# One ring of four PSUM banks for the maximum tiles and the side jobs, and whole value products between groups of tiles, in an attention and feed-forward kernel

## The reference, cut to what matters

```python
hid = _group_norm(xr, norm_w, norm_b)                      # 32 groups
qkv = jnp.einsum('oc,bcl->bol', qkv_w, hid) + qkv_b[None, :, None]
...
weight = jnp.einsum('bhct,bhcs->bhts', q * scale, k * scale)
weight = jax.nn.softmax(weight.astype(jnp.float32), axis=-1)
a = jnp.einsum('bhts,bhcs->bhct', weight, v)
h = jnp.einsum('oc,bcl->bol', proj_w, a.reshape(b, c, L)) + proj_b[None, :, None]
x = x + h.reshape(b, c, hh, ww)
...
h = gelu(rmsnorm2d(x, norm1_w)); x = x + conv1x1(h, conv_w, conv_b)
h = rmsnorm2d(x, norm2_w);       h = gelu(conv1x1(h, ffn_w1, ffn_b1))
x = x + conv1x1(h, ffn_w2, ffn_b2)
```

## Time and profile before

| | |
|---|---|
| median of 3 runs | 1712.55 us (1711.57 to 1712.57) |
| the profiled execution | 1714.98 us, its span 1713.0 us |
| mean granted TensorE clock | 0.984 |
| TensorE busy (matmuls) | 1675.6 us, 98% |
| VectorE busy | 1460.5 us, 85% |
| ScalarE busy | 1367.4 us, 80% |
| GpSimd busy | 337.3 us, 20% |

### The profile page before, as it was taken

The page is one execution under the profiler, slowest core; times in us unless marked ns, Lnnn a source line. Parts: engine busy times, 40 slices in busy tenths (PEclk is TensorE's granted clock), DMA queues, the critical chain, the costliest instruction groups (busy, mean ns, idle before and its releaser), DMA issues.

```text
span 1713.0 us, 33562 instructions
## 1 busy us (share of the span) xinstructions
PE 1675.6 (98%) x12522; PEld 678.8 (40%) x12522; DVE 1460.5 (85%) x2415; ACT 1367.4 (80%) x2478; POOL 337.3 (20%) x411
## 2 busy tenths in 40 slices
PE   5999999999999999999999999999999999899999
PEld 2433333333333333333333333333333333455555
DVE  4999999999999999999999999999999995455552
ACT  2388888888888888888888888888888888666664
POOL 3101111111111111212121212121211113222220
PEclk9699999999999999999999999999999998999999
DMA  6133333333333334343333333233333320333332
GB/s 117 27 46 58 58 58 59 58 58 58 57 59 55 61 54 62 52 62 54 61 55 59 57 58 58 46 59 46 58 45 58 46 60 21 94 104 96 102 109 74
DMA packets 58625, 106.16 MB, mean 62 GB/s; under 512 B 32864, under 2 KB 33632, under 8 KB 58464
## 3 DMA queue, kind: packets, MB, share of 16 engines
q1 hardware_dynamic: 56160, 95.64, 32.7%
q10 hardware_dynamic: 2304, 8.39, 1.3%
HBM read 34.48 MB, written 9.05 MB: 25 GB/s over the span
## 4 chain that ended last, share of the span: by engine, by line
PE 96%; DVE 2%; SPq 0%; issue 0%; POOL 0%; ACT 0%; DMA 0%; DVEq 0%; POOLq 0%; ACTq 0%
PE psum L696 33%; PE psum L667 27%; PE psum L680 14%; PE psum L773 7%; PE psum L578 4%; PE psum L744 2%; PE psum L746 2%; PE psum L745 2%; PE psum L570 2%; PE psum L623 2%; DVE maxes L1022 1%; PE psum L781 1%; PE psum L591 0%; PE psum L601 0%; DVE k_high L1112 0%
## 5 line engine op out<-in xcount | busy, mean ns | idle before, releaser
L1022 DVE TENSOR_REDUCE maxes<-psum 128x1 f32<-128x512 f32 x2048 | 1276.8, 683 | 93.7 <-PE psum L667 91.7
L915 ACT ACTIVATE probs<-psum 128x512 f32<-128x512 f32 x2048 | 1110.0, 597 | 218.1 <-PE psum L680 194.5
L667 PE MATMUL psum<-k_stack,q_stack 62*128 62x512 f32 x2048 | 771.3, 456 | 1.7 <-DVE maxes L1022 0.9
L680 PE MATMUL psum<-q_stack,k_stack 64*128 64x512 f32 x2048 | 752.8, 452 | 0.0
L696 PE MATMUL psum<-probs,values 128*32 128x256 f32 (+1 forms) x7040 | 624.7, 427 | 0.7 <-ACT probs L915 0.6
L667 PEld LDWEIGHTS psum<-k_stack,q_stack 62*128 62x128 f32 x2048 | 317.0, 187 | 506.8 <-DVE maxes L1022 421.4
L680 PEld LDWEIGHTS psum<-q_stack,k_stack 64*128 64x128 f32 x2048 | 305.1, 185 | 12.3 <-issue 6.1
L696 PEld LDWEIGHTS psum<-probs,values 128*32 128x32 f32 x7040 | 138.7, 108 | 317.0 <-issue 232.6
L773 PE MATMUL psum<-probs,first_weights 128*128 128x512 f32 x256 | 116.6, 598 | 0.9 <-DVE raw L1190 0.9
L434 POOL CAST parts<-neg_max 128x16 fp32r<-128x16 f32 x64 | 12.6, 197 | 528.3 <-DVE neg_max L1001 528.3
L924 ACT ACTIVATE probs<-psum,params_sb 128x512 f32<-128x512 f32 x128 | 82.1, 686 | 20.9 <-PE psum L746 14.7
(11 more groups left out here) (95 smaller groups left out, 965.9 us busy)
## 6 DMA issues: line engine op xcount, KB each, us to landing
q_stack<-q_high SPq DMA_DIRECT2D x128, 128.0 KB, 3.9
k_stack<-k_high SPq DMA_DIRECT2D x128, 128.0 KB, 5.2
values<-inv_rms_rows SPq DMA_DIRECT2D x32, 512.0 KB, 5.0
x_sb<-in_x SPq DMA_DIRECT2D x16, 512.0 KB, 7.2
q_stack<-q_low SPq DMA_DIRECT2D x64, 128.0 KB, 6.3
k_stack<-k_low SPq DMA_DIRECT2D x64, 128.0 KB, 7.0
q_stack<-rows SPq DMA_DIRECT2D x512, 2.0 KB
attn<-raw SPq DMA_DIRECT2D x128, 64.0 KB, 2.3
```

Source lines behind the costliest of these rows:

```text
L667: nc.tensor.matmul(psum[:, BANKS + tile % BANKS, :], q_stack[used, place, p, chunk % 4, chunk // 4, :], k_stack[used, place, p, HALF * key ...
L680: nc.tensor.matmul(psum[:, tile % BANKS, :], k_stack[used, place, p, 128 * chunk:128 * chunk + 128], q_stack[used, place, p, :, t, :], sta ...
L915: nc.scalar.activation(probs[:, tile % 8, :], psum[:, tile % BANKS, :], ACT.Exp, scale=SCALE).then_inc(probs_ready, 1)
L1022: nc.vector.tensor_reduce(maxes[:, chunk // 4, j, 4 * p + chunk % 4, key_half:key_half + 1], psum[:, BANKS + max_tile(u, s, k) % BANKS, :] ...
```

## The change

The side jobs lose bank 7 of their own. Banks 3, 4, 5 and 7 become one ring of four, and M tiles and side jobs take its places in the order in which TensorE issues them (`max_place`, `job_place`); each waits for whatever reads the place four before. S tiles keep their three banks. In `slot` the order of a step is now one of four, by `s % 4`; side jobs keep their steps and stand behind two pairs at odd steps. The value product is whole in three of four orders and split in the fourth (`s % 4 == 3`). On ScalarE a side job's copy moves from behind the fourth exponential to behind the second. Before the first M tile TensorE now waits for the copies of image 1's first products (`c == PROLOGUE - 1`). The diff, cut to its core:

```diff
+        RING_BANKS = (3, 4, 5, 7)
+        max_place, job_place, freed = {}, {}, []
+        def side_job_read(b, half, s):
+            at = (half, s)
+            if at == LAST_K and PROLOGUE <= b + 1 < IMAGES:
+                return qk_full, 4 * (b + 1) + 4
...
+            return None
+        for u in range(-1, UNITS):
+            for s in range(STEPS):
+                for k in range(4):
+                    if k == 2 and u >= 0 and side_job_read(u // 2, u % 2, s) is not None:
+                        job_place[u // 2, u % 2, s] = len(freed)
+                        freed.append(side_job_read(u // 2, u % 2, s))
+                    if 0 <= max_tile(u, s, k) < UNITS * TILES:
+                        max_place[max_tile(u, s, k)] = len(freed)
+                        freed.append((max_taken, max_tile(u, s, k) + 1))
+        def bank_of(n):
+            return psum[:, RING_BANKS[n % len(RING_BANKS)], :]
+        def job_bank(b, half, s):
+            return bank_of(job_place[b, half, s]) if b >= 0 else misc
...
+                if c >= PROLOGUE:
+                    wait_for_place(job_place[(c - 1, *VALUES[part])])
                 for k in range(4):
                     chunk = 4 * part + k
-                    last = nc.tensor.matmul(misc[:, 128 * k:128 * k + 128], hid[:, 128 * chunk:128 * chunk + 128],
-                                            wv[:, :], start=True, stop=True)
+                    last = nc.tensor.matmul(values_bank(c, part)[:, 128 * k:128 * k + 128],
+                                            hid[:, 128 * chunk:128 * chunk + 128], wv[:, :], start=True, stop=True)
                 last.then_inc(v_ready, 1)
...
-                if (half, s) == VALUES[0] and b + 1 >= PROLOGUE and has_image(b + 1):
-                    if has_image(c):
+                if (half, s) == GROUP_VAR and has_image(c):
+                    pe.wait_ge(gn_mix, b + 3)
+                    if b >= 0:
+                        wait_for_place(job_place[b, half, s])
+                    else:
                         pe.wait_ge(mean_taken, b + 3)
-                    values_of(b + 1, 0)
-                if (half, s) == GROUP_VAR and has_image(c):
-                    at_least(pe, mean_taken, b + 3)
-                    at_least(pe, v_full, b * 2 + 3)
-                    pe.wait_ge(gn_mix, b + 3)
-                    nc.tensor.matmul(misc[:, 0:1], group_mean[:, :], g_mix, start=True, stop=True).then_inc(gn_group, 1)
...
+                    if c == PROLOGUE - 1:
+                        pe.wait_ge(qk_full, c * 4 + 4)
+                        pe.wait_ge(v_full, c * 2 + 2)
...
-            def wait_for_bank(tile, freed):
-                at_least(pe, freed, tile - BANKS + 1)
+            def wait_for_place(n):
+                if n >= len(RING_BANKS):
+                    signal, value = freed[n - len(RING_BANKS)]
+                    pe.wait_ge(signal, value)
...
-                wait_for_bank(tile, probs_ready)
+                at_least(pe, probs_ready, tile - BANKS + 1)
...
-                    middle = 2 if s % NK == 1 and not broken else 1
-                    for k in range(4):
-                        maximum_scores(u, s, k)
-                        if has_unit(u):
-                            scores(u, 2 * parity + half, s, k)
-                        if k == 1 and (broken or b < 0):
-                            side_jobs(b, parity, half, s)
-                        if k == middle and not broken:
-                            weigh_before(u, parity, half, s, 0, QUARTER)
-                    weigh_before(u, parity, half, s, 0 if broken else QUARTER, HALF)
+                    if s % 4 == 0:
+                        scores(u, place, s, 0)
+                        maximum_scores(u, s, 0)
+                        maximum_scores(u, s, 1)
+                        scores(u, place, s, 1)
+                        scores(u, place, s, 2)
+                        maximum_scores(u, s, 2)
+                        side_jobs(b, parity, half, s)
+                        weigh_before(u, parity, half, s, 0, HALF)
+                        scores(u, place, s, 3)
+                        maximum_scores(u, s, 3)
+                    if s % 4 == 1:
+                        maximum_scores(u, s, 0)
+                        scores(u, place, s, 0)
+                        scores(u, place, s, 1)
+                        maximum_scores(u, s, 1)
+                        side_jobs(b, parity, half, s)
+                        maximum_scores(u, s, 2)
+                        scores(u, place, s, 2)
+                        scores(u, place, s, 3)
+                        maximum_scores(u, s, 3)
+                        weigh_before(u, parity, half, s, 0, HALF)
+                    if s % 4 == 2:
+                        maximum_scores(u, s, 0)
+                        scores(u, place, s, 0)
+                        scores(u, place, s, 1)
+                        maximum_scores(u, s, 1)
+                        maximum_scores(u, s, 2)
+                        scores(u, place, s, 2)
+                        side_jobs(b, parity, half, s)
+                        weigh_before(u, parity, half, s, 0, HALF)
+                        scores(u, place, s, 3)
+                        maximum_scores(u, s, 3)
+                    if s % 4 == 3:
+                        scores(u, place, s, 0)
+                        maximum_scores(u, s, 0)
+                        maximum_scores(u, s, 1)
+                        scores(u, place, s, 1)
+                        side_jobs(b, parity, half, s)
+                        weigh_before(u, parity, half, s, 0, QUARTER)
+                        maximum_scores(u, s, 2)
+                        scores(u, place, s, 2)
+                        scores(u, place, s, 3)
+                        maximum_scores(u, s, 3)
+                        weigh_before(u, parity, half, s, QUARTER, HALF)
...
-                    side_jobs(b, parity, half, s)
+                        if k == 1:
+                            side_jobs(b, parity, half, s)
...
-                                                psum[:, BANKS + max_tile(u, s, k) % BANKS, :],
+                                                bank_of(max_place[max_tile(u, s, k)]),
```

More of the change, by code:

```diff
@@ L276, in image_of_x @@
             return x[:, one(b), lo:lo + n].squeeze(1)
+        RING_BANKS = (3, 4, 5, 7)
[4 more added lines that the diff above has]
+                return qk_full, 4 * (b + 1) + 4
+            if at == GROUP_MEAN and b + 2 < IMAGES:
+                return mean_taken, b + 3
+            if at == GROUP_VAR and b + 2 < IMAGES:
+                return gn_var, b + 3
+            if at in VALUES and PROLOGUE <= b + 1 < IMAGES:
+                return v_full, 2 * (b + 1) + VALUES.index(at) + 1
+            if at == FIRST_SUMS and b == IMAGES - 1:
+                return sums_taken, 1
+            if at in PROJ and 0 < b < IMAGES:
+                return proj_taken, (b - 1) * NT + PROJ.index(at) + 1
+            if half == 1 and s in QK_STEPS and PROLOGUE <= b + 2 < IMAGES:
+                return qk_full, 4 * (b + 2) + QK_STEPS.index(s) + 1
+            return None
[12 more added lines that the diff above has]
+            return bank_of(job_place[b, half, s]) if b >= 0 else misc
         block = ctx.enter_context(nc.Block())
@@ L602, in side_jobs @@
-                if (half, s) == VALUES[1] and b + 1 >= PROLOGUE and has_image(b + 1):
-                    if has_image(c):
-                        pe.wait_ge(gn_var, b + 3)
-                    pe.wait_ge(v_full, b * 2 + 3)
-                    values_of(b + 1, 1)
+                    if b >= 0:
+                        wait_for_place(job_place[b, half, s])
+                    else:
+                        at_least(pe, v_full, 2 * (b + 2))
+                    nc.tensor.matmul(job_bank(b, half, s)[:, 0:1], group_mean[:, :], mean_var[:, 0:1],
+                                     start=True, stop=True).then_inc(gn_mean, 1)
@@ new lines, in side_jobs @@
+                if (half, s) == GROUP_VAR and has_image(c):
+                    pe.wait_ge(gn_mix, b + 3)
+                    if b >= 0:
+                        wait_for_place(job_place[b, half, s])
+                    else:
+                        pe.wait_ge(mean_taken, b + 3)
+                    nc.tensor.matmul(job_bank(b, half, s)[:, 0:1], group_mean[:, :], g_mix,
+                                     start=True, stop=True).then_inc(gn_group, 1)
+                for part in range(2):
+                    if (half, s) == VALUES[part] and PROLOGUE <= b + 1 < IMAGES:
+                        values_of(b + 1, part)
@@ L624, in side_jobs @@
+                        nc.tensor.matmul(job_bank(b, half, s), wp[:, :], attn[:, HALF * t:HALF * t + HALF],
                                          start=True, stop=True).then_inc(proj_ready, 1)
@@ L633, in side_jobs @@
                     values_of(c, 1)
-                if half == 1 and s in QK_STEPS and c >= PROLOGUE and has_image(c):
```

(16 more changed lines are left out.)

64 lines of the change are left out of this document (23 added, 41 removed).

## The result

| | before | after |
|---|---|---|
| median (lowest to highest) of 4 runs each | 1712.56 us (1711.57 to 1716.71) | 1672.08 us (1670.55 to 1672.58) |
| the profiled execution, its span | 1714.98 us, 1713.0 us | 1672.58 us, 1670.6 us |
| mean granted TensorE clock | 0.984 | 0.983 |

The ratio is 0.9758, with a 95% interval of 0.9740 to 0.9775: 40.5 us less, where the forecast had 32 less (1680.5).

A forecast was written before the change was run, and what follows sets the result against it. TensorE was taken as the bound, without gaps. Net 2.5 us per full image, 35.3 in all with images 0, 14 and the last, less 2.3 and 0.8, made 32.2: 1680.5 us from the median 1712.55, range 1666 to 1699.

The forecast's parts named there:

- Fewer splits and longer groups: TensorE in attention: 14 fewer split value products save 2.1 us per image, groups of three pairs 3.4, together 5.5.
- The split product waits for ScalarE: Steps with s % 4 == 3: the split product waits 0.31 us for an exponential at six places, 1.9 us per image.
- rival 4: Waits hide: exponentials come 0.03 us sooner, no loss at the copies; 3.5 us saved per image, 1667 us; chance 0.10.
- The accumulator's copy together with a side job's: ScalarE: both copies in one step make the next group's third S tile late, four times, 1.1 us per image.
- Images 0 and 14: Images with only five side jobs each: predicted to gain 0.6 us (image 0) and 1.2 us (image 14).
- The last 13 steps: S tiles running alone at the end: three per group against three banks wait for exponentials, costing 2.3 us, bounds 0 and 5.5.
- The start: First M tile waits for the copy ending at 37.57 + 0.59, so it starts 0.75 us later; counted as 0.8.
- Rival 1: TensorE: a third pair's loads stay bare, so it adds 0.34 us, not 0.23; no change, 1714.5 us; chance 0.08.
- rival 2: The loop S, exponential, S becomes the bound; 0.12 us more erases the gain, 0.2 more gives 1736 us; chance 0.07.

The follow-up runs named there:

- the kernel with two halves: Changed kernel with each whole value product issued as two halves of 256 columns directly behind each other: 1672.13 us, ratio 0.9748 to the kernel before.

## Why the prediction was right, and which of its terms was off

**Fewer splits and longer groups, 5.5 us per image: right.** 24 whole and 8 split products stand in the image, third pairs come 0.24 behind the second, groups of three take 0.90. Two halves in a row cost what a whole product does, so the 0.15 of a split is the change of kind. All of this rests on M's fourth place: with the old banks the same order keeps 1.1.

**The split product waits for ScalarE, 1.9: right.** It waits 0.28 (1.18 less 0.90), six times an image, 1.7 us in all. Behind group mean or variance there is no wait, as predicted:

```profile
843.19 0.38 PE L647 MATMUL psum<-gn,first_weights 128*128 128x1 f32 x2
843.50 0.64 PE L730 MATMUL psum<-probs,values 128*32 128x256 f32 x8
```

The loop was 1.18 and not 1.21, since the exponential began 0.53 behind its S, which here stands ahead of its M; rival 4 had reckoned with 0.03 less.

**The accumulator's copy together with a side job's, 1.1: the term that was mis-sized.** The prediction let the exponential follow the side job's copy by the copy's whole 0.69. It follows after 0.57 (786.81 to 787.38), and after 0.57 to 0.59 wherever the copy is of queries, keys or a projection: here ScalarE starts an instruction before the one ahead of it has ended (exponentials take 0.60 and follow at 0.49). The accumulator's copy takes 0.46 and not 0.49. So the third S tile's bank comes free about when it is due. Three such steps per image take 2.35 us instead of 2.24; the fourth, whose side job is the shorter copy of values (0.59), loses nothing. That is 0.3 per image, not 1.1. With the 0.2 from the split waits the net is 5.5 - 1.7 - 0.3 = 3.5, not 2.5; measured are 3.4.

The trace of before could mislead here. An exponential did start 0.69 behind such a copy there, but it was waiting for its own S tile, 0.56 behind that tile's start. Timeline of ScalarE and TensorE, before:

```profile
823.08 0.69 ACT L865 ACTIVATE q_full<-psum,params_sb 128x512 f32<-128x512 f32 x1
823.77 0.60 ACT L915 ACTIVATE probs<-psum 128x512 f32<-128x512 f32 x1
823.21 0.73 PE L680 MATMUL psum<-q_stack,k_stack 64*128 64x512 f32 x2
```

Between 300 and 1300 us every exponential of before that follows a copy of queries, keys or a projection waited like this, so the trace did not show the spacing by itself. The accumulator's copy did: 0.59 long, the next exponential 0.47 behind its start. The duration had been used where the spacing belonged, though for exponentials and reductions the text had kept them apart.

Over the 13 images the gain is 11.3 us above the forecast, and the two spans are 10.2 further apart than the 32.2 forecast. By the medians the miss is 8.4, since the profiled run of before was 2.4 above its median and that of after only 0.5.

**Images 0 and 14: too little by 1.2 together.** Image 0 was given only 0.6 for VectorE's sake and gained 1.4; image 14 gained 1.6 and not 1.2.

**The last 13 steps, 2.3: about right.** 1.8 by the trace without the step s = 6, and the old order in these steps takes 1.4 of it back.

**The start, 0.8: right for the wait; the rest changes between runs.** In the profiled run the first M starts 2.76 later (40.22 against 37.46). Timeline where the M tiles begin:

```profile
39.53 0.59 ACT L940 COPY values<-psum 128x512 f32<-128x512 f32 x1 [1.25 <-PE psum L617]
...
40.22 0.73 PE L699 MATMUL psum<-k_stack,q_stack 62*128 62x512 f32 x4 [0.72 <-issue]
```

M starts 0.69 behind the start of the last copy; before it started 0.11 ahead of it, so the wait costs 0.80. The same 0.68 to 0.69 stands in all nine profiles with this wait, and the 0.11 ahead comes back in both that have it moved (37.69 against 37.80, 36.88 against 36.98). The other 1.96 are the copy itself, which is later than before (39.53 against 37.57). In the nine profiles it starts anywhere from 37.24 to 39.53, at 38.15 in the second run of this very kernel, and 37.24 is earlier than before. So this part belongs to the run and not to the change; what moves it is open.

**Where rivals stood.** Rival 1 is refuted: the third pair uses the same rows as the second, its loads run while the second's products do, and it adds 0.24, not 0.34. The rule of the Trainium skill ("TensorE: Matmul & The Clock Gate", Part 3) that a load overlaps a running product only where the row groups differ does not hold for these tiles; the measurement decides. The point at which rival 2 decides, 0.12 more on ScalarE's loop, was not reached; the loop got shorter. Rival 4 had the mechanism nearest to what happened, and at 1667 it lies 5 us below the result, the forecast 8 above. But its 3.5 per image is a slip: its own terms (2.5, six times 0.03, and 1.1) make 3.8, which is about 1663 and 9 below, so the two were about equally far off. The loss at the copies did not vanish, as rival 4 had it, but fell to 0.3. VectorE is the next limit in sight: 81.27 of 83.70.

## What to carry to other kernels

A fixed cost that is paid per group of like products is lowered by longer groups, up to what the buffers carry: compare the pace of the tiles (0.24 to 0.34 here) with the consumer's pace and its full loop (0.49 and 1.18 on ScalarE, 0.61 a tile on VectorE), and look first to the slower consumer for the spare buffer. (Here the spare bank went with the side jobs' places, so the two were not tried apart.) If short jobs join such a ring, their readers must come early in their own queue: the order with early copies alone was worth 0.3% here, the ring with early copies alone nothing, order and ring with late copies nothing, and the three together 2.4%. Price what follows an instruction by the spacing between starts, not by its duration.

## What the runs showed of the hardware

A copy that takes 0.71 on ScalarE lets the next exponential start after 0.57. And in the last unit TensorE's granted clock is at the lower of its levels after a pause, for a time that differs between runs of the same kernel. First the changed kernel's timeline of TensorE there, then its windows, then those of its second run:

```profile
1385.34 0.76 PE L814 MATMUL psum<-q_stack,wconv_high 128*128 128x512 f32 x1 [3.29 <-DVE q_stack L1172]
...
1390.37 1.94 PE L730 MATMUL psum<-probs,values 128*32 128x512 f32 x8
1392.23 0.79 PE L714 MATMUL psum<-q_stack,k_stack 64*128 64x512 f32 x1
```

```profile
1386.00:1393.00 7.00, 7.00 (x23) 2.89 (x24) 2.64 (x3) 5.03 (x9) 0.00 (x0) 0.50 0.00 0
1394.00:1402.00 8.00, 7.36 (x49) 3.00 (x41) 4.40 (x5) 5.00 (x10) 2.94 (x2) 1.00 0.02 2
```

```profile
1385.00:1393.00 8.00, 8.00 (x26) 2.85 (x25) 2.56 (x3) 5.44 (x9) 0.00 (x0) 0.50 0.00 0
1393.00:1395.50 2.50, 2.50 (x9) 1.50 (x6) 0.89 (x2) 0.00 (x0) 0.00 (x0) 0.50 0.00 0
```

The pause was 3.29 us in both runs. In the first it ended at 1385.34, and from 1394 on the clock is full; in the second it ended at 1384.13, and the clock is still at 0.50 up to 1395.5. At 0.50 of the clock (1.2 GHz) a whole value product takes 1.86 us (1390.37 to 1392.23) instead of 1.00. The step s = 6 of this unit, in which this falls, took 7.47 us in the one run and 8.80 in the other, and 5.43 in the kernel with two halves, a spread larger than what the start and the last steps are worth. Differences of 1 to 2 us between two single profiles of this kernel mean little before that step, and the place of the last copy of the start, are taken out.
